# First layer's cross attention in steps of two heads: scores on half the rows each, three score banks, two product banks

## What is computed

```
xn = layer_norm(x, gamma_pt)
q, k, v, ff = split(xn @ w_fused, [H*DH, H*DH + DH, H*DH + 2*DH])   # one k and one v for all heads
q, k = rope(q), rope(k);  q = q * DH**-0.5
out = softmax(causal(q k^T)) v
y = x + out @ w_attn_out + silu(ff_gate) * ff_val @ w_ff_out
yn = layer_norm(y, gamma_ca);  ctx = layer_norm(context, gamma_ctx)
cq = (yn @ w_q) per head * DH**-0.5;  ck, cv = split(ctx @ w_kv)    # one ck and one cv for all heads
cout = softmax(cq ck^T) cv
fv, fg = split(yn @ w_ff1)
z = y + cout @ w_out + silu(fg) * fv @ w_ff2
```

## Times and profile before

| | |
|---|---|
| times | 3669.17 us (median of 3; 3668.32 to 3670.8) |
| the profiled execution | 3673.39 us, of which the span of the trace is 3671.6 us |
| PE busy | 3435.7 us (94% of the span) |
| DVE busy | 1881.6 us (51%) |
| ACT busy | 1912.8 us (52%) |
| POOL busy | 397.5 us (11%) |
| first layer | the first 1.1 ms, 8 turns of some 134 us |
| cross attention of a turn | 42 us |

### The profile page before, as it was taken

How to read it: one execution, slowest core, us unless ns; L and a number is a source line. 1 busy time by engine, 2 the same in 40 slices (tenths; PEclk the granted TensorE clock), 3 DMA queues, 4 the chain that set the end, 5 groups by cost and what they waited for, 6 DMA issues and landing times. The chain is left out here.

```text
span 3671.6 us, 67713 instructions
## 1 busy us (share of the span) xinstructions
PE 3435.7 (94%) x21748; PEld 2524.7 (69%) x21748; DVE 1881.6 (51%) x5735; ACT 1912.8 (52%) x5549; POOL 397.5 (11%) x488
## 2 busy tenths in 40 slices
PE   8999999999997999999988999999999998798887
PEld 6778778778775666666656666667666675565665
DVE  3654654644644444455544554455445444656655
ACT  3553543544544555656644554555555454366666
POOL 2101101101102111001101000000000000211111
PEclk9999999999998999999999999999999999899999
DMA  6000000000004000000001000000000000000000
GB/s 207 4 12 15 4 12 15 4 12 15 4 3 150 14 8 5 13 13 13 13 6 55 9 8 11 8 12 9 8 15 9 8 10 14 12 18 22 13 27 5
DMA packets 58462, 75.11 MB, mean 20 GB/s; under 512 B 6752, under 2 KB 55584, under 8 KB 57024
## 3 DMA queue, kind: packets, MB, share of 16 engines
q1 hardware_dynamic: 58176, 71.45, 6.3%
HBM read 64.04 MB, written 7.40 MB: 19 GB/s over the span
## 5 line engine op out<-in xcount | busy, mean ns | idle before, releaser
L161 PE MATMUL l_bank<-l_xT,weights_of_layers_and 128*128 128x224 f32 x2816 | 616.7, 371 | 14.8 <-ACT l_xT L1143 8.0
L161 PEld LDWEIGHTS l_bank<-l_xT,weights_of_layers_and 128*128 128x128 f32 x2816 | 542.4, 199 | 58.4 <-ACT l_xT L1143 8.7
L389 ACT ACTIVATE l_pT<-l_bank 125x336 f32<-125x336 f32 (+2 forms) x736 | 347.6, 472 | 321.1 <-PE l_bank L319 310.8
L319 PEld LDWEIGHTS l_bank<-identity,l_p 112*125 112x125 f32 (+2 forms) x2336 | 332.1, 177 | 198.6 <-issue 112.0
L319 PE MATMUL l_bank<-identity,l_p 112*125 112x112 f32 (+2 forms) x2336 | 387.7, 278 | 36.2 <-ACT l_p L363 30.8
L406 ACT ACTIVATE l_p<-l_p,l_nm 112x375 f32<-112x375 f32 x384 | 233.2, 607 | 234.3 <-DVE l_nm L444 233.0
L161 PE MATMUL l_bank<-weights_of_layers_and,l_cT 128*125 128x256 f32 (+2 forms) x960 | 303.8, 454 | 13.6 <-DVE l_queries_or_hidden L1845 9.3
L161 PE MATMUL l_bank<-l_cT,weights_of_layers_and 128*128 128x375 f32 x832 | 304.0, 494 | 0.0
L710 POOL TENSOR_TENSOR l_ve<-l_mv,eps 112x2 f32<-112x2 f32 (+1 forms) x89 | 17.3, 195 | 2438.8 <-DVE l_mv L704 2438.8
L402 ACT ACTIVATE l_p<-l_p,l_nm 112x112 f32<-112x112 f32 x512 | 192.2, 377 | 149.4 <-DVE l_nm L440 130.8
L341 PEld LDWEIGHTS l_bank<-l_pT,l_cv 125*64 125x64 f32 (+1 forms) x3648 | 162.8, 130 | 137.0 <-issue 97.0
(11 more groups left out here) (255 smaller groups left out, 5887.4 us busy)
## 6 DMA issues: line engine op xcount, KB each, us to landing
l_cT<-in_ctx_turned SPq DMA_DIRECT2D x32, 375.0 KB, 3.5
l_cx<-in_ctx SPq DMA_DIRECT2D x16, 375.0 KB
context_rows<-in_ctx_reversed SPq DMA_DIRECT2D x16, 375.0 KB
tokens<-x_after_layer SPq DMA_DIRECT2D x25, 224.0 KB, 2.5
x_after_layer<-l_z SPq DMA_DIRECT2D x24, 224.0 KB, 2.4
weights_of_layers_and<-bias_lines_kept SPq DMA_DIRECT2D x1, 2625.0 KB, 15.6
weights_of_layers_and<-in_L_xattn_w_fused SPq DMA_DIRECT2D x1, 2048.0 KB, 10.9
weights_of_layers_and<-in_L_xattn_w_ff SPq DMA_DIRECT2D x1, 2048.0 KB, 12.8
```

What stands on the lines that cost most here:

```text
L161: last = pe.matmul(out, left, right, start=(k == 0), stop=(k == len(pairs) - 1))
L319: last = pe.transpose(TR.bank(m)[:ph.keys, g * ph.rows:(g + 1) * ph.rows], p[:ph.rows, m % self.p_slots, g * ph.keys:(g + 1) * ph.keys], i ...
L389: return act.activation(out, src, ACT.Copy)
```

## The change

`Part` gets a number `abreast`, 1 by default and 2 for the cross attention of the first layer. In an even step PE does, for the pair of items that begins there, the waits of both items and then both score products one after the other; the transposes, and ACT's copies of them, are done for two items together, in the step in which the second one's turn comes (one step later than before for the first of the two). In an odd step neither is done. The score products read only the 64 partitions of their own head, of queries and of keys, so the zeros are no longer read; the two products of a pair lie on different halves of the rows of the array and go to different banks. DVE's and ACT's work per item, and the order of maxima and exponentials, stay as they are. The banks are dealt out anew: three for scores (0 to 2), two for turned probabilities (3 and 4), one for outputs (5), two for projections (6 and 7). All other users of `Part` keep `abreast` at 1, where the code does what it did.

```diff
     def __init__(self, name, items, dh, rows, q, k, val, ready, val_ready, place, out, bias=None, grouped=False, sides=2, tiles=CT,
-                 turned_by="act", emptied_by="dve", scaled_by="dve", ring=None):
+                 turned_by="act", emptied_by="dve", scaled_by="dve", ring=None, abreast=1):
+        self.abreast = abreast
...
+    def abreast_of(self, k):
+        n = self.abreast
+        return range(k - n + 1, k + 1) if k % n == n - 1 else ()
...
         def scores(ph, k):
-            m = ph.first + k
-            for sem, count in S.free(i, m, *ph.ready(k)):
-                pe.wait_ge(sem, count)
+            own = ph.abreast_of(k + ph.abreast - 1)
             width = ph.keys * ph.tiles
-            for g in range(ph.n):
-                last = pe.matmul(S.bank(m)[:ph.rows, g * width:(g + 1) * width], ph.q(k, g), ph.k(k, g), start=True, stop=True)
-            last.then_inc(S.full.sem, 1)
+            for n in own:
+                for sem, count in S.free(i, ph.first + n, *ph.ready(n)):
+                    pe.wait_ge(sem, count)
+            for n in own:
+                for g in range(ph.n):
+                    last = pe.matmul(S.bank(ph.first + n)[:ph.rows, g * width:(g + 1) * width], ph.q(n, g), ph.k(n, g), start=True, stop=True)
+                last.then_inc(S.full.sem, 1)
 
         def turns(ph, k):
-            m = ph.first + k
-            for sem, count in TR.free(i, m, self.scaled[ph.scaled_by].this(ph.scaled0 + k)):
-                pe.wait_ge(sem, count)
...
+            for n in ph.abreast_of(k):
+                m = ph.first + n
+                for sem, count in TR.free(i, m, self.scaled[ph.scaled_by].this(ph.scaled0 + n)):
+                    pe.wait_ge(sem, count)
...
         def turned(ph, k):
             if ph.turned_by == "act":
-                self.turned_copy(act, i, ph, k, copy)
+                for n in ph.abreast_of(k):
+                    self.turned_copy(act, i, ph, n, copy)
...
         def cross_q(k, g):
             j, m, a = cross_at(k)
-            return rows_of[:, j, ROWS * m:ROWS * (m + 1)]
+            return rows_of[64 * a:64 * a + 64, j, ROWS * m:ROWS * (m + 1)]
+
+        def cross_k(k, g):
+            j, m, a = cross_at(k)
+            return ckz[64 * a:64 * a + 64, j, a, :]
...
+        cross = Part("c", PAIR * 2 * TILES, DH, ROWS, cross_q, cross_k, lambda k, g, t: cv[:, cross_at(k)[0], t, :],
+                     cross_ready, cross_values_ready, cross_place, cross_out, abreast=2)
...
-        P = Ring(ctx, nc, "l0_product", banks[5:8], jobs)
-        O = Ring(ctx, nc, "l0_output", banks[4:5], own.output_jobs() + cross.output_jobs())
-        A = Columns(ctx, nc, "l0", [own, cross], banks[0:2], banks[2:4], O, 3, LAG_VALUES, 4, 4)
+        P = Ring(ctx, nc, "l0_product", banks[6:8], jobs)
+        O = Ring(ctx, nc, "l0_output", banks[5:6], own.output_jobs() + cross.output_jobs())
+        A = Columns(ctx, nc, "l0", [own, cross], banks[0:3], banks[3:5], O, 3, LAG_VALUES, 4, 4)
```

More of the change, by code:

```diff
@@ L305, in scores @@
         def scores(ph, k):
-            m = ph.first + k
-            for sem, count in S.free(i, m, *ph.ready(k)):
-                pe.wait_ge(sem, count)
+            own = ph.abreast_of(k + ph.abreast - 1)
             width = ph.keys * ph.tiles
-            for g in range(ph.n):
-                last = pe.matmul(S.bank(m)[:ph.rows, g * width:(g + 1) * width], ph.q(k, g), ph.k(k, g), start=True, stop=True)
-            last.then_inc(S.full.sem, 1)
-        def turns(ph, k):
-            m = ph.first + k
-            for sem, count in TR.free(i, m, self.scaled[ph.scaled_by].this(ph.scaled0 + k)):
-                pe.wait_ge(sem, count)
[L318 to L321, removed]
+            for n in own:
[5 more added lines that the diff above has]
+                last.then_inc(S.full.sem, 1)
+        def turns(ph, k):
+            for n in ph.abreast_of(k):
+                m = ph.first + n
+                for sem, count in TR.free(i, m, self.scaled[ph.scaled_by].this(ph.scaled0 + n)):
+                    pe.wait_ge(sem, count)
+                for g in range(ph.n * ph.tiles):
+                    last = pe.transpose(TR.bank(m)[:ph.keys, g * ph.rows:(g + 1) * ph.rows], p[:ph.rows, m % self.p_slots, g * ph.keys:(g + 1) * ph.keys],
+                                        ident[:ph.rows, :ph.rows])
+                last.then_inc(TR.full.sem, 1)
         def values(ph, k):
@@ L461, in turned @@
             if ph.turned_by == "dve":
-                self.turned_copy(dve, i, ph, k, copy)
+                for n in ph.abreast_of(k):
+                    self.turned_copy(dve, i, ph, n, copy)
         def outputs(ph, k):
@@ L897, in layer0 @@
                    bias=lambda k: wide(c.causal[:T, :], 1, G), grouped=True, scaled_by="pool")
-        cross = Part("c", PAIR * 2 * TILES, DH, ROWS, cross_q, lambda k, g: ckz[:, cross_at(k)[0], cross_at(k)[2], :], lambda k, g, t: cv[:, cross_at(k)[0], t, :],
-                     cross_ready, cross_values_ready, cross_place, cross_out)
+        cross = Part("c", PAIR * 2 * TILES, DH, ROWS, cross_q, cross_k, lambda k, g, t: cv[:, cross_at(k)[0], t, :],
+                     cross_ready, cross_values_ready, cross_place, cross_out, abreast=2)
         beside_own = {s: [(f"f{s}", "dve")] for s in range(8)}
```

## The result

| | before | after |
|---|---|---|
| median of the runs | 3669.99 us (4) | 3699.95 us (4; 3693.41 to 3706.69) |
| profiled execution, span | 3673.39, 3671.6 us | 3695.53, 3693.8 us |
| PE busy | 3435.7 us (94%) | 3400.1 us (92%) |

The ratio of after to before is 1.0079, with a 95% interval of 1.0066 to 1.0093. The profiled executions differ by 22.2 us, the medians by 30.

What follows compares the result with a forecast made beforehand. PE was taken to bound both attentions before, a loop through DVE and ACT cross attention after. Terms in us: -3 + 7.6 + 3.4 + 2.8 + 5 = +15.8, from 3669.2 to 3685; range 3675 to 3697.

Steps and rivals of the forecast that it cites:

- the ten pairs behind them: Cross attention after the first values: ten pairs would go from 29.9 to 28.8 us a turn.
- xT: Cross attention, step 25: xT would delay the copies behind it (two activations) by .4 us.
- q0 waits for v0, z1 for q0: Projection banks: q0 .3 us late behind v0's copy, z1 .1 behind q0; 7 times .4, 2.8 us.
- cT01 waits for f7: Projection banks: cT01 waits until f7 is emptied, making y0 .42 us late, 8 times: 3.4 us.
- Passes in pairs: Cross attention scores: passes of two heads run together, a pair taking .63 us instead of 1.26.
- The loop: Cross attention: a loop through scores, maxima, exponentials, copies and values, not PE, sets 2.79 us a pair.
- The rival without the loop: Cross attention: PE stays the bound at 2.42 us a pair, 3655 us in all; chance .15.
- A layout step: PE in cross attention: one more change of layout a pair, costing .10 us, between 0 and .20.
- The gain of the cross attention's steps: Cross attention as a whole: a gain of .4 us a turn, 3 us in all.
- f0's wait: Turn's start: f0 waits for q3's bank, starting 1.36 us late; 1.1 late in effect, 7 boundaries, 7.6 us.
- cf2 to cf7: Projection jobs, each waiting for the one two before: no cost, or .15 us a job if misread.
- The clock: PE's clock falls to its lower level at three of seven turn boundaries: 5 us, between 0 and 12.

Runs made afterwards that it cites:

- e3: The changed kernel with both maxima of a pair back to back on DVE and the scaling of the item before behind them; 3698.47 us, ratio 1.0075.
- e9: The changed kernel with DVE's order altered: scaling of the item before first, then both maxima of the new pair; 3669.13 us, ratio 0.9988.
- e2: The changed kernel with an empty job in the projection ring, so that f0 takes q2's bank and does not wait for q3; 3697.37 us, ratio 1.0073.
- e8: The kernel before, with only q3's products made to wait until z1 is emptied; 3686.32 us, ratio 1.0040.
- e4: The changed kernel with score products reading all 128 partitions again, its order and banks kept; 3702.58 us, ratio 1.0092.
- e13: The changed kernel run again unaltered for a second profile; 3698.52 us, ratio 1.0072.
- e1: The kernel before with only the changed kernel's banks (three for scores, two for projections); 3727.89 us, ratio 1.0162.

## Why the prediction came out as it did

**Direction and mechanism held in the main.** Slower, by banks, with cross attention unable to use what the half rows save. I forecast 15.8 us more; it is 22 by the profiled executions and 30 by the medians. The 3700 lies within the range of 3655 to 3705, but above the 3675 to 3697 that the terms were given. By its own steps, us a turn, without falls:

| step | predicted | measured |
|---|---|---|
| cross attention, up to the first values | 0 | +.13 |
| the ten pairs behind them | -1.1 | -.57 |
| xT | +.4 | +.45 |
| last transposes uncovered behind z0 | +.33 | +.32 |
| q0 waits for v0, z1 for q0 | +.4 | +.46 |
| turn's start | +1.1 | +1.27 |
| cT01 waits for f7 | +.42 | +.28 (.37 at y0's start) |
| the jobs behind yT, to the scores | 0 | +.33 |
| sum | +1.5 | +2.7 (A + B: +2.7) |

- **Passes in pairs: right.** Four rows in .90 us, two and two, in steps of .42 and .41, where I had .32. The rule of the Trainium skill, "TensorE: Matmul & The Clock Gate", section "Part 3: Packing small matmuls", that MATMULs keep program order, does not describe these fp32 products: the second head's first pass starts 7 ns after the first head's first and .41 before the first head's second.
- **The loop: right, to .03.** 2.815 a pair, 2.79 predicted. From scores to values 3.97 (3.91): max after .93 (.83), second max .99 (.99), exponential .57 (.59), copy .57 (.56), values .91 (.94). Then .81 and .85 to scores (1.67). The rival without the loop falls by e3 and e9.
- **A layout step costs more than .10.** PE's own work for a pair is 2.49 to 2.58, 2.42 predicted: scores to values .83 for .73, transposes to scores up to .94 for .86. The loop hides it.
- **The gain of the cross attention's steps was mis-sized: nothing, not .7 a turn.** Up to the last values ahead of z0 the stage is as long as before (45.54 for 45.53). The ten pairs took 29.30 us (before 29.87; I had 28.8). DVE's measuring and centring of x turned intervals of 2.49 into 3.50 and 3.78: over ten pairs at 2.815 they leave 1.15 us, where I had .9. I had said that the loop's slack takes up a third of the 1.55 us of delay; it took up a quarter. This .25, another .25 from 2.815 for 2.79, .13 at the start and .05 at xT make the .7.
- **f0's wait: there, but not alone; that 1.27 came out near my 1.1 is luck.** By itself it costs 1.17 (the last start, up to the first transposes). At starts with a branch 1.12 to 1.16 of the 1.27 stay when it is taken away (e2). I listed who waits for z1's bank by when PE's array comes to q3, and left out that PE's sequencer runs ahead: its wait holds up the loop's branch. e8 prices that at 1.48 where there is a branch and 0 where there is none, e2 shows the two covering each other. The idle time of .53 that the earlier trace rows put down to "issue" was its trace in the kernel before, and I had read it as nothing. Since the scores ahead of f0 are late too, the idle time just before f0 is .40 at these starts and not 1.4, and 1.96 at the last; its releaser is the one that I named (L1309, now L1323).
- **cT01: nearly as forecast,** .39 idle for .5, ended by DVE's line on f7; y0 is .37 late, and .09 of this comes back within y0. **cf2 to cf7: put at nothing, .33 measured.** By the starts of the 80 passes two of the six jobs wait, cf2 and cf4, at .125 each, near the bound of .15 a job that I gave; the last .08 is the step to the scores, which now changes the layout.
- **The clock: 5 in the sum, 5.5 net, by luck** over the first layer up to the last cross scores (after 3 turns of 3.5, before 3 of 1.7). I counted three starts of seven, and there were three, but each was followed by a second fall at the wait for yT, the kind that before has in three turns too. I had put nine passes into a fall where the earlier trace rows show 11; the 1.7 us for one is what B shows. In other executions there are more, and by the two profiles these make up most of the distance from 22 to 30.

How the terms add up to the 22.2: six turns at 2.66 are 16.0, the last turn 2.3, the first own attention 1.4, falls 5.5, together 25.2 at the last cross scores. Behind these after is 3.0 shorter, by nothing that the change does: 1.1 in the third layer, most of it at the one branch there that takes .24 us and leaves PE no idle time, and the rest in the fourth, where the falls of the clock lie otherwise in the two executions.

## What to carry to other kernels

When work is taken from an engine, sum the loop through the others first: here three quarters of what PE saved in a pair (.4 us, of which .1 arrived) became idle time. With DVE's order changed and the banks left alone the same half rows made a kernel faster than both (3658.6 us). A bank taken from a ring is paid for at the waits that the engine's sequencer meets ahead of its work, so look at what stands behind them in program order, a loop's branch above all. Two late causes at one place cover each other; take each away alone, and both, before saying which one costs.

## What the hardware showed that I had not expected

- The closing branch of the first and third layers' loops takes 3.3 to 4.8 us in PE's sequencer, in all kernels here (.21 to .25 in the shorter loops of the other two), and is hidden only if the sequencer reaches it early enough. The length varies from turn to turn in the same execution.
- At turn starts with a branch where PE had been idle for .81 us or less, the clock never fell in 30; at those with 1.3 to 2.9 it fell in 27 of 48, within 2 us of PE's return. Neither the idle time nor the branch's length says which: e4 has six with 1.6 to 2.3 and none fell. At last starts, without a branch, it fell in three of the six where f0 waits 1.96 us (e3, e9, e13), and in none of the seven others. A fall at a start costs 1.4 to 2.6 us, one behind yT 1.7. Why it comes in some turns and not in others stays open.
- In one kernel (e1) the same instructions of a later layer got 3.3 to 4.2 us of idle time behind the branch, for 1.0 or less in the others. Its cause stays open.
